# A four-layer vision model on one core: stores of the Mamba phase on ScalarE's DMA queue, tap loads in 8 transfers, last columns kept by ScalarE

## What is computed

```python
# projection to 48 + 48 channels, 3x3 depthwise convolution, gate
xz = einsum('bld,ed->ble', u, in_w);  xm, z = split(xz, 2)
xm = silu(conv1d(xm, 3 taps) + c1_b)
dbl = einsum('bld,ed->ble', xm, xp_w)          # 3 + 16 + 16 rows
dt = softplus(einsum('blr,dr->bld', dbl[:3], dt_w) + dt_b)
A = -exp(A_log)
def step(h, inp):                              # over 3136 pixels
    da = exp(dt_t[..., None] * A)
    h = da * h + (dt_t * x_t)[..., None] * B_t[:, None, :]
    y = einsum('bdn,bn->bd', h, C_t)
y = (ys + xm * Dp) * silu(z)
```

## Time and profile before

| | before |
|---|---|
| median of 3 runs | 4458.61 us (4454.52 to 4467.43) |
| the profiled execution | 4458.26 us |
| its span | 4456.6 us |
| granted TensorE clock, mean | 0.931 |
| busy: PE, DVE, ACT, POOL | 82%, 65%, 60%, 36% of the span |
| Mamba phase, first DMA to last scan | 1022.7 to 2600 us |

### The profile page before, as it was taken

One profiled execution on the slowest core, in us unless ns is written; L12 is line 12 of the kernel. 1 busy time (PEld: TensorE's weight loads), 2 busy tenths in 40 slices (PEclk: granted clock), 3 DMA queues, 4 the chain that ended last, 5 costly groups with the idle time before them and its releaser, 6 DMA issues. The chain is left out here.

```text
span 4456.6 us, 73149 instructions
## 1 busy us (share of the span) xinstructions
PE 3640.5 (82%) x20680; PEld 2121.9 (48%) x20680; DVE 2888.3 (65%) x4570; ACT 2692.4 (60%) x4664; POOL 1600.1 (36%) x1447
## 2 busy tenths in 40 slices
PE   4899999785677888888876658689999786799956
PEld 2788888442233333333332214344444332799932
DVE  2666666671289989898999937566666665111146
ACT  4555555695666767676765328677777576233346
POOL 0333333101366767676766630045555400000000
PEclk9999999897889989999999979899999988899979
DMA  3000000123536364646544122100000022100012
GB/s 92 19 15 14 14 14 14 35 57 99 152 102 162 116 177 116 172 125 166 152 135 129 52 69 50 39 16 15 15 15 15 9 53 71 34 11 11 11 44 53
DMA packets 203144, 296.59 MB, mean 67 GB/s; under 512 B 68686, under 2 KB 188670, under 8 KB 202242
## 3 DMA queue, kind: packets, MB, share of 16 engines
q1 hardware_dynamic: 193798, 285.57, 24.4%
q10 hardware_dynamic: 9216, 9.65, 0.9%
HBM read 193.01 MB, written 102.03 MB: 66 GB/s over the span
## 5 line engine op out<-in xcount | busy, mean ns | idle before, releaser
L1570 POOL TENSOR_TENSOR mam_hc<-mam_h,mam_cs 128x896 f32<-128x896 f32 x336 | 712.5, 2126 | 333.4 <-DVE mam_h L1513 317.3
L1301 PE MATMUL mam_ps_y<-mam_hc,mam_ident 128*128 128x448 f32 x1344 | 628.4, 595 | 211.0 <-POOL mam_hc L1570 211.0
L1513 DVE TENSOR_TENSOR_SCAN mam_h<-mam_a,mam_kept,mam_dbx 128x448 f32<-128x448 f32 x672 | 729.3, 1123 | 1.2 <-ACT mam_a L1417 1.2
L1417 ACT ACTIVATE mam_a<-mam_ft,mam_a_neg 128x448 f32<-128x448 f32 x672 | 402.1, 656 | 242.4 <-DVE mam_h L1513 241.8
L1944 POOL TENSOR_TENSOR scan_ch<-scan_h,scan_cs 128x392 f32<-128x392 f32 x256 | 344.2, 1360 | 560.8 <-DVE scan_h L1910 560.8
L1301 PEld LDWEIGHTS mam_ps_y<-mam_hc,mam_ident 128*128 128x128 f32 x1344 | 261.3, 204 | 550.0 <-POOL mam_hc L1570 330.7
L1500 DVE TENSOR_TENSOR mam_dbx<-mam_ps_u,mam_bs 128x448 f32<-128x448 f32 x672 | 381.8, 611 | 92.5 <-DMA mam_cs<-dram_bc 91.1
L756 POOL TENSOR_TENSOR att_prob<-att_prob,att_share 128x588 f32<-128x588 f32 x128 | 151.9, 1186 | 452.1 <-DVE att_share L941 452.1
L1910 DVE TENSOR_TENSOR_SCAN scan_h<-scan_turned_in,scan_start 128x392 f32<-128x392 f32 x192 | 256.6, 1356 | 25.6 <-ACT scan_turned_in L1829 24.2
L1784 PE MATMUL scan_ps_merged<-scan_ch,scan_w_merge 128*128 128x392 f32 x512 | 230.6, 532 | 47.8 <-POOL scan_ch L1944 46.0
L2034 PE MATMUL lstm_ps<-lstm_hs,lstm_w_h 128*128 (+1 forms) x1344 | 264.9, 352 | 0.0
(11 more groups left out here) (215 smaller groups left out, 7984.1 us busy)
## 6 DMA issues: line engine op xcount, KB each, us to landing
mam_taps<-normed SPq DMA_DIRECT2D x1008, 43.5 KB
mam_bs<-dram_bc SPq DMA_DIRECT2D x28, 896.0 KB, 11.6
mam_cs<-dram_bc SPq DMA_DIRECT2D x28, 896.0 KB, 16.9
mam_ft<-dram_steps SPq DMA_DIRECT2D x42, 448.0 KB, 5.1
normed<-f_staged SPq DMA_DIRECT2D x384, 38.1 KB
f_mixed<-mixed SPq DMA_DIRECT2D x384, 36.8 KB
dram_gs<-mam_gs SPq DMA_DIRECT2D x56, 224.0 KB, 2.7
mam_gt<-dram_gs SPq DMA_DIRECT2D x56, 224.0 KB
```

The source lines that it names most:

```text
L1301: mm = pe.matmul(ps_y[p % 2][:, 0:MT], ident[:], hc[t % 2][:, i, :], start=False, stop=(t % 8 == 7 and i == 1))
L1417: act.activation(a[t % 3][:, i, :], ft[p % 2][:, 0, :], ACT.Exp, scale=a_neg[:, at:at + 1]).then_inc(decays, 1)
L1513: dve.tensor_tensor_scan(h[:, n % 8, :], a[t % 3][:, i, :], dbx[:, i, 0:MT], kept[:, at:at + 1], ALU.mult, ALU.add).then_inc(scanned, 1)
L1570: pool.tensor_tensor(hc[t % 2][:], h[:, row:row + 2, :], cs[:, 2 * pair:2 * pair + 2, :], ALU.mult).then_inc(weighed, 1)
```

## The change

Four things, all in the Mamba phase:

- The 18 tap transfers of an item become 8. Each takes one to three neighbouring shifts of one kernel row at once, through a source pattern whose outermost dimension is the shift: `[[1, n], [PADDED, C], [1, TAP_N]]` with n = 3, 2, 1 and 3 for each image. The bytes are the same. On the SBUF side the rows are 72, 48, 24 and 72 partitions.
- `store_xm`, `store_zs` and `store_gs` (five transfers) move from slot 5 of SyncE to slot 4 of ScalarE, behind the step size.
- `save`, the copy of last columns, moves from VectorE to ScalarE, behind the decays of step t, and for step t - 3; VectorE's scan of step t then waits for that copy instead of one 45 steps older.
- GpSimd's `carry` of an item (two copies of two columns) moves from slot 1 of the next item to slot 4 of the item's own front.

```diff
                     for i in range(2):
-                        for tap in range(TAPS_5 + TAPS_4):
-                            at = (8 * s + tap // 3) * PAD + tap % 3
-                            tile, row = ((taps_5, tap) if tap < TAPS_5
-                                         else (taps_4, tap - TAPS_5))
-                            sp.dma_start(tile[m % 2][i][C * row:C * row + C, :],
-                                         normed[2 * q + i, :, at:at + TAP_N]
+                        for tile, row, dy, dx, n in ((taps_5, 0, 0, 0, 3), (taps_5, 3, 1, 0, 2),
+                                                     (taps_4, 0, 1, 2, 1), (taps_4, 1, 2, 0, 3)):
+                            shifted = bass.AP(
+                                tensor=normed.tensor,
+                                offset=(2 * q + i) * C * PADDED + (8 * s + dy) * PAD + dx,
+                                ap=[[1, n], [PADDED, C], [1, TAP_N]])
+                            sp.dma_start(tile[m % 2][i][C * row:C * (row + n), :], shifted
                                          ).then_inc(taps_in[m % 2], 16)
...
-                        if k == 5 and inner is not None:
-                            store_xm(inner)
-                            store_zs(inner)
-                        if k == 5 and front is not None:
-                            store_gs(front)
...
-                        pe.wait_ge(taps_in[m % 2], 288 * (m // 2 + 1))
+                        pe.wait_ge(taps_in[m % 2], 128 * (m // 2 + 1))
...
+                def keep_rows(dram, tile, m, sem):
+                    s, q = divmod(m, DUOS)
+                    for i in range(2):
+                        lanes = 8 * (2 * q + i)
+                        act.dma_start(dram(s)[:, lanes:lanes + 8, :],
+                                      tile[HALF * i:HALF * i + D, :]).then_inc(sem, 16)
...
+                def store_gs(m):
+                    act.wait_ge(silu_b, m + 1)
+                    act.dma_start(gs_d[m], gs[:]).then_inc(gs_out, 16)
...
+                def save(t):
+                    p, pair = divmod(t, 8)
+                    at = p % DB * STATES + 2 * pair - 2
+                    row = (2 * t - 2) % 8
+                    act.wait_ge(scanned, 2 * t + 2)
+                    act.activation(kept[:, at:at + 4], h[:, row:row + 4, MT - 1], ACT.Copy
+                                   ).then_inc(saved, 1)
...
                             decay(t)
+                        if t % 2 == 0 and 0 <= t - 3 < STEPS:
+                            save(t - 3)
...
                         if k == 4 and inner is not None:
                             step_logs(inner)
+                            store_xm(inner)
+                            store_zs(inner)
+                        if k == 4 and front is not None:
+                            store_gs(front)
...
                         if t % 2 == 0:
-                            reached(dve, saved, (t - 48) // 2 + 1)
+                            reached(dve, saved, t // 2 - 1)
...
-                        if k == 1 and inner is not None:
-                            carry(inner)
+                        if k == 4 and front is not None:
+                            carry(front)
```

More of the change, by code:

```diff
@@ L1122, in keep_rows @@
                                      tile[HALF * i:HALF * i + D, :]).then_inc(sem, 16)
[L1124 to L1130, removed]
                 def store_dt(m):
@@ L1134, in store_dt @@
                     keep_rows(lambda s: steps_d[s, :, :, 0, :], dt, m, dt_out)
-                def store_gs(m):
-                    sp.wait_ge(silu_b, m + 1)
-                    sp.dma_start(gs_d[m], gs[:]).then_inc(gs_out, 16)
                 def store_bc(m):
@@ L1408, in take_result, with store_xm, store_zs @@
                     act.activation(res[r % 2][:], ps_c[0:HALF, 0:MT], ACT.Copy).then_inc(taken, 1)
+                def keep_rows(dram, tile, m, sem):
[4 more added lines that the diff above has]
+                                      tile[HALF * i:HALF * i + D, :]).then_inc(sem, 16)
+                def store_xm(m):
+                    act.wait_ge(silu_m, m + 1)
+                    keep_rows(lambda s: steps_d[s, :, :, 1, :], xm, m, xm_out)
+                def store_zs(m):
+                    act.wait_ge(silu_z, m + 1)
+                    keep_rows(lambda s: zs_d[s], zs, m, zs_out)
+                def store_gs(m):
+                    act.wait_ge(silu_b, m + 1)
+                    act.dma_start(gs_d[m], gs[:]).then_inc(gs_out, 16)
                 def decay(t):
@@ L1515, in scan @@
                                            ).then_inc(scanned, 1)
-                def save(t):
-                    p, pair = divmod(t, 8)
-                    at = p % DB * STATES + 2 * pair - 2
-                    row = (2 * t - 2) % 8
-                    dve.wait_ge(scanned, 2 * t + 2)
-                    dve.tensor_copy(kept[:, at:at + 4], h[:, row:row + 4, MT - 1]
-                                    ).then_inc(saved, 1)
                 def times_z(p):
@@ L1548, in _ @@
                             drive(t, 1)
-                        if t % 2 == 0 and 0 < t <= STEPS:
-                            save(t - 1)
                         if t % 8 == 3 and 0 <= t // 8 - 1 < PASSES:
@@ L1599, in _ @@
                 for j in range(FIRST, LAST):
-                    inner, previous = item(j + LEAD - 1), item(j + LEAD - 2)
+                    front, inner = item(j + LEAD), item(j + LEAD - 1)
+                    previous = item(j + LEAD - 2)
                     for k in range(6):
```

## The result

| | before | after |
|---|---|---|
| median | 4457.66 us (4454.52 to 4467.43) | 4591.34 us (4582.31 to 4592.99) |
| ratio, with its 95% interval | | 1.0292 (1.0271 to 1.0313) |
| profiled execution, its span | 4458.26, 4456.6 us | 4592.48, 4590.8 us |
| granted TensorE clock, mean | 0.931 | 0.915 |

What follows compares the result with a forecast made beforehand. VectorE was taken to bound the recurrence, with a ScalarE-TensorE chain just as long. Fill +60, steps 0 to 53 +1, full stretch +150 and last stretch -34 gave +177 on 4458.3: 4635 us, range 4470 to 4820.

Steps and rivals of the forecast that it cites:

- Packets to engines: Tap loads: outermost DRAM count sets the engines, so 3 or 2 instead of 12; small packets per fill item near 94.
- An engine's rate: DMA engine 0 was taken to move 21 GB/s, between 16.5 under load and 25 alone; fill needs 429 KB an item.
- bound at 25 GB/s: Up to the first scan: lighter bound of the +60 us term, +21 us if an engine moves 25 GB/s.
- The sign that would show it: TensorE would wait hundreds of us for taps, 9.2 before; DMA share stuck near 3/16 for long times in the fill.
- theory B: Formed after the trace: ScalarE's chain of 27 us paces the full stretch; undo_taps expected at about 4548 us.
- The issues on ScalarE: Five stores issued behind the step size cost ScalarE about 2.9 us an item, bounds 1.1 and 3.4.
- Rival 1: Taps cost nothing and only ScalarE's chain is left: +20 us, 4478 us; chance 0.16 (with rival 4, engines in turn).
- Steps 0 to 53: Nine items after the first scan: engine 0 needs 25.1 us an item, 12 us of first loads remain: +1 us.
- The full stretch: Steps 54 to about 276, 37 items: chain 27.6 us plus 1.5 for stage boundaries an item: +150 us.
- The copies: Last stretch: moving the copies off VectorE saves 34 us.
- a copy's wait on ScalarE: ScalarE's copy waits only as the decays ahead already did, and VectorE needs it two steps later; +0.2 us an item.
- The carry: Fill: made an item earlier, it removes TensorE's wait for GpSimd's copies, some 4.5 us of a 15.4 us item.

Runs made afterwards that it cites:

- 31 rows against 32: Changed kernel plus two unread loads per item into spare partitions of `taps_4`: with 31 rows each 4709.40 us, with 32 rows each 4597.26 us.
- undo_taps: Changed kernel with the old 18 tap transfers of 24 rows put back: 4511.91 us, ratio 1.0107 to the kernel before.
- carry_alone: Kernel before with only GpSimd's earlier carry: 4443.67 us, ratio 0.9950 to the kernel before.
- undo_stores: Changed kernel with the five stores back on SyncE, taps still in 8 transfers: 4533.14 us, ratio 1.0145 to the kernel before.
- copies_carry: Kernel before with only the copies on ScalarE and the earlier carry (18 taps, stores on SyncE): 4413.46 us, ratio 0.9889.
- wide_and_between: Changed kernel with 8 tap transfers channel outermost (12 engines) and one store behind each step-size activation on ScalarE: 4376.28 us, ratio 0.9810 to the kernel before.
- stores_between: Changed kernel with 18 taps and the five ScalarE stores placed one behind each step-size activation: 4379.46 us, ratio 0.9825 to the kernel before.

## Why the prediction was right, and where its sizes were off
The sign, the time (4591 in a range of 4470 to 4820) and the two mechanisms held. That the sum is only 43 us off is in part luck: by stretch the forecast was 26, 49 and 13 us too high and once 22 too low. Point by point:

**Packets to engines: right.** 95 small packets an item, no window of the item read above under the share of two engines, and 31 rows against 32 are the direct proof.

**An engine's rate: the mis-sized term.** I took 21 GB/s, between 16.5 and 25. It was 24.4 to 25.0 (the prediction's own rows add up to 432 KB, not 429, which makes it 24.6 to 25.2). Two or three engines with 24 rows at a stretch go at the speed of the lone engine of the earlier trace rows. Why the 16 are slower under load (two rows at a stretch, or all at once) was not tried. Of the +34 up to the first scan, eight items of the fill are 8 x 2.2 = +17. Another +15 lie before them, where I had counted 5 for the first taps: TensorE waits 12.12 us for the first pair's taps, 6.78 before, and 4.66 instead of 1.41 for the second. The prediction's bound at 25 GB/s, redone, is 18 + 4 + 5 = +27, where it says +21.

**The sign that would show it: wrong.** I said that TensorE would wait hundreds of us for taps; it waits 21. The taps are loaded an item early. What is late is the small thing behind them: `gs` goes over all 16 engines, and ScalarE's wait is for all of its parts. It lands in 7.3 us in the fill, 2.7 before, 4.2 in undo_taps and 4.3 in carry_alone: about 3 us are the concentration's, and the rest came with the early carry. The DMA share was not stuck near 3/16 (0.19) either: two of the eight windows of the item above lie below that, the others between 0.21 and 0.55. Someone who looked only at waits for taps would have put the taps' price too low, as I did in theory B. It took undo_stores, where the taps' wait is 89.6 us, and the runs with 31 and 32 rows to put that right.

**The issues on ScalarE: right,** 2.83 to 2.87 us where 2.9 stood, and the chain is 27.8 us in the item above and 27.3 an item in undo_taps, boundaries included (27.6 forecast). Rival 1, without the taps' price, had 1016 us for steps 54 to 275; undo_taps has 1011.6.

**Steps 0 to 53: the step that failed.** I counted engine 0 and the first loads, +1, and took the issues to matter only through the results' chain. But the decays stand behind the issues as well, and VectorE waits for them directly: 7 times, 20.9 us in this stretch. undo_taps, with the stores alone, needs 13.9 us more than copies_carry here (247.1, 233.2), the changed kernel 26. The taps' 12 us are mostly VectorE's waits for `bs` and `cs`, 24.5 us after and 13.6 in undo_taps.

**The full stretch: +101, not +150.** It was forecast as 27.6 us an item by the chain and 1.5 for the boundaries, with engine 0 at 27.4 just below. The median item took 27.0, and the mean 27.9, so the boundaries came to 0.9 an item: half of the excess is the chain's, half the boundaries'. Engine 0 was no second pace of 27.4; within a stage it cost nothing. That its load would be felt beside `bs` and `cs` was right, but it came by another path too. I had SyncE gain by fewer issues, 3 to 6 us for eight. At the boundaries they took some 21 and 14 us in two items in a row, where the eighteen took some 8 and 11 in undo_taps. VectorE waits for `bs` and `cs` 55.6 us in this stretch, 56.6 before: the group behind the taps waits 14.23 us at 1721.94, where it waited 8.87, but the first group's wait is gone.

**The copies: -21, not -34.** They left VectorE, but it then reaches the last stage's rows early. VectorE's groups in the last stretch of copies_carry:
```profile
L1511 DVE TENSOR_TENSOR mam_dbx<-mam_ps_u,mam_bs 128x448 f32<-128x448 f32 x120 | 68.7, 619 | 4.2 <-DMA mam_cs<-dram_bc 4.0
...
L1539 DVE SCALAR_TENSOR_TENSOR mam_dt<-mam_ln,mam_consts,mam_es 128x448 f32<-128x448 f32 x1 | 1.5, 1477 | 2.5 <-issue 2.5
```
These are 6.7 us of waiting, where there were 0.3 before, and the stretch is 23.6 us shorter (225.4, 201.8). The stretch holds 29 copies, not 30, and from the start of each to the start of the next instruction they took 30.2 us: the 32.9 count twice where neighbours overlap. 30.2 less 6.4 of new waiting are the 23.8 that were gained. After, VectorE waits 8.9 us here.

The prediction also said that a copy's wait on ScalarE would be hidden, because VectorE needs it two steps later. That step failed: in the changed kernel scans wait 37.1 us over 38 times for a copy, in undo_taps 39.3, in copies_carry 8.3 over 10, before never. The copy stands behind the decays, and where the issues make these late it is late as well. What the copies would bring without that wait no run tells, since none leaves them on VectorE beside the moved stores. A wait of 1.8 us "issue" stands before the step size in every item of the full stretch once the copies are away (66.1 us over 40 times after; 13.5 over 8 before); what holds VectorE there, the trace doesn't show, and no run here settles it.

**The carry: its own gain was overstated.** The wait of 4.5 us an item went as forecast, but in carry_alone the first scan starts only 14 us earlier (1189.9, 1204.0), 3 of which lie before the phase's first table load (1019.5, 1022.7), and the whole run gains 0.5%. I had not asked what is late next: SyncE's queue.

## What to carry to other kernels
Before fewer and larger transfers replace many, look at which dimension stands outermost on the DRAM side: its count decides how many DMA engines work, and a swap of two dimensions was worth some 85 us here. The price of a crowded engine can show up in another transfer's landing, not in the one that crowds (`gs` here, `bs` and `cs` at the boundaries), and in the length of its own issues. And a mean over a stretch hides where a price stands: cut it into items before naming what sets the pace. An issue on ScalarE's queue was free behind an activation about as long as itself, and cost its full length behind another issue: spread them.

## What the hardware showed that was not expected
- 31 rows instead of 32, fewer bytes, cost 112 us: one engine instead of 16.
- A DMA engine's rate: 17 GB/s in the fill before, 24.4 to 25.0 with 24 and 31 rows at a stretch.
- A longer wait of TensorE goes with a slower projection behind it. From 1150 us on, the projection into `ps_a` takes 871 ns a matmul after and 864 in undo_taps, behind waits of 5.5 us, 737 in wide_and_between, behind waits half as long. Between 1200 and 2500 us the changed kernel runs 36 of its 46 groups of four such matmuls at the half clock, behind a mean wait of 5.3 us. The kernel before runs 13 of 44 so, behind 2.6 us, and 23 at the full clock, behind 1.3 us; waits of 2 to 3 us stood ahead of both. The mean clock is 0.915 after, 0.931 before and 0.938 in stores_between.
